# A convolution pass whose sums, stores and loads are spread over a group's steps, with the images turned first

## The reference

```python
x = x + _L0_conv_ref(_gn(x), weight, bias_term)     # depthwise 31x31, padding 15
x = x + _L1_conv_ref(_gn(x), ...)                   # window attention (7x7 windows) and an MLP
```

## Time and profile before

| | us |
|---|---|
| median of 3 runs | 5388.03 (5382.51 to 5395.19) |
| the profiled execution | 5403.44 |
| its span | 5401.6 |
| its convolution pass, until the last copy `inner` | 1191.2 |

### The profile page before, as it was taken

One profiled execution on the slowest core, in us unless ns is written; L12 is line 12 of the kernel. 1 busy time (PEld: TensorE's weight loads), 2 busy tenths in 40 slices (PEclk: granted clock), 3 DMA queues, 4 the chain that ended last, 5 costly groups with the idle time before them and its releaser, 6 DMA issues.

```text
span 5401.6 us, 225369 instructions
## 1 busy us (share of the span) xinstructions
PE 4898.2 (91%) x94576; PEld 3759.4 (70%) x94576; DVE 3825.5 (71%) x6236; ACT 3718.6 (69%) x5686; POOL 3389.0 (63%) x4559
## 2 busy tenths in 40 slices
PE   7999999987999999999999999999999999999998
PEld 6999999974666666666666666666666666666665
DVE  6888887864777776777777777777766777677774
ACT  5676766655777777777677777777766777677775
POOL 2111111114777777777777777777777777777774
PEclk9999999995999999999999999999999999999997
DMA  8888888865666666666666666666666666666662
GB/s 190 202 202 205 198 201 199 201 141 112 137 142 137 144 137 141 139 142 137 143 134 141 138 143 138 142 137 142 138 139 133 140 142 138 138 137 142 136 141 53
DMA packets 1168755, 802.28 MB, mean 149 GB/s; under 512 B 454404, under 2 KB 1142628, under 8 KB 1167652
## 3 DMA queue, kind: packets, MB, share of 16 engines
q1 hardware_dynamic: 1167748, 787.87, 66.7%
HBM read 470.41 MB, written 317.17 MB: 146 GB/s over the span
## 4 chain that ended last, share of the span: by engine, by line
PE 46%; ACT 16%; issue 9%; DVE 6%; ACTq 0%; POOL 0%; DVEq 0%; POOLq 0%
PE ps_ring L1219 9%; PE ps_pv L1152 6%; ACT L899 6%; PE ps_ring L1089 4%; PE ps_xc L1194 4%; PE ps_t L1106 4%; PE ps_ring L1211 4%; PE ps_s L1106 3%; ACT b_lg L856 3%; ACT b_mid L884 3%; PE ps_ring L1091 3%; DVE b_h L1002 3%; DVE b_rest L1013 3%; PE ps_ring L1090 3%; ACT b_rstd L861 2%
## 5 line engine op out<-in xcount | busy, mean ns | idle before, releaser
L970 DVE TENSOR_REDUCE b_mx<-ps_s 113x12 f32<-113x588 f32 x1024 | 780.8, 762 | 160.3 <-PE ps_s L1106 160.0
L869 ACT ACTIVATE b_probs_t<-ps_t 128x588 f32<-128x588 f32 x1024 | 667.0, 651 | 329.0 <-PE ps_t L1106 328.9
L775 POOL TENSOR_TENSOR b_mid_lo<-b_mid,b_mid_hi 128x392 fp32r<-128x392 f32 x768 | 788.0, 1026 | 43.2
L1152 PEld LDWEIGHTS ps_pv<-b_vd,b_probs_t 128*49 128x49 f32 x24576 | 614.9, 127 | 162.4 <-issue 153.4
L1152 PE MATMUL ps_pv<-b_vd,b_probs_t 128*49 128x18 f32 x24576 | 665.7, 200 | 0.3 <-issue 0.3
L830 POOL TENSOR_TENSOR b_outs<-b_y,b_xs 96x392 f32<-96x392 f32 x256 | 317.2, 1239 | 444.7 <-DVE b_y L1051 444.7
L856 ACT ACTIVATE b_lg<-ps_ring,b_cols 96x392 f32<-96x392 f32 x512 | 299.1, 584 | 383.4 <-PE ps_ring L1098 380.4
L1008 DVE TENSOR_TENSOR b_sq_lo<-b_sq,b_sq_hi 96x392 fp32r<-96x392 f32 x256 | 289.3, 1130 | 332.0 <-ACT b_sq_hi L877 332.0
L258 POOL TENSOR_TENSOR xd<-xt 128x448 f32<-128x448 f32 x96 | 112.1, 1168 | 649.0 <-DVE xt L409 649.0
L884 ACT ACTIVATE b_mid<-ps_ring,b_cols 128x392 f32<-128x392 f32 x768 | 424.2, 586 | 135.1 <-PE ps_ring L1091 132.1
L817 POOL TENSOR_SCALAR b_planes<-b_rest 96x784 bf16<-96x784 f32 x256 | 216.3, 845 | 421.9 <-DVE b_rest L1017 421.9
(11 more groups left out here) (166 smaller groups left out, 14196.1 us busy)
## 6 DMA issues: line engine op xcount, KB each, us to landing
stacked_qk<-b_planes SPq DMA_DIRECT2D x512, 220.5 KB, 3.0
b_q_st<-stacked_qk SPq DMA_DIRECT2D x512, 220.5 KB, 4.4
b_k_st<-stacked_qk SPq DMA_DIRECT2D x512, 220.5 KB, 5.7
toep<-filters_padded SPq DMA_DIRECT2D x96, 936.5 KB, 7.0
stacked_qk<-b_planes SPq DMA_DIRECT2D x512, 147.0 KB, 2.3
gtoep<-filters_summed SPq DMA_DIRECT2D x96, 624.5 KB, 9.3
stacked_qk<-b_planes SPq DMA_DIRECT2D x512, 73.5 KB, 1.9
b_xs<-x_scratch SPq DMA_DIRECT2D x224, 147.0 KB, 2.9
```

What stands on the lines that cost most here:

```text
L775: pool.tensor_tensor(mid_lo[:, m, :], mid[:, m, :], mid_hi[:, m, :].bitcast(F32), ALU.subtract).then_inc(S["mid_split"], 1)
L869: act.activation(pt[:, p, :].rearrange("k (e n) -> k e n", e=2), ps_t[:, :, 0:HPAIR * TOK], ACT.Exp, scale=float(DH) ** -0.5).then_inc(S[" ...
L970: dve.tensor_reduce(mx[0:rows_q, :].rearrange("q (e m p) -> q e m p", e=2, p=PAIRS)[:, :, :, p], ps_s[0:rows_q, :, 0:HPAIR * TOK].rearrang ...
L1152: ins = pe.matmul(to, pt[:, p, at:at + TOK], vd[:, m % VR, p, h, :, :], start=True, stop=True, skip_group_check=True)
```

## The change

In `conv_pass` alone:

- **ScalarE.** `stats` makes one pass for each call. The values of `xin` are summed when k = 3g-5, the squares when k = 3g-4; the values of `x1t` when k = 3g+3, the squares when k = 3g+4. Each pass now counts on `sums_done` or `sums1_done`, so those who wait for them count to twice the number.
- **SP.** The stores of a group are issued when k = 3g+4 instead of 3g+3. The loads stay where they are.
- **VectorE.** The images of channel k+2 are turned at the head of the step. The variance stands ahead of the low halves of the filters, and the shift `aff` between the two.
- **POOL.** `xd` is formed of channel k+2, a step earlier.
- **Filter semaphores.** The second filter counts on its own semaphore, `g_loaded`, and ScalarE waits for it only before its rounding.

```diff
             def load_filter(c):
...
-                for pad, dst, n in ((wpad, toep, TLEN), (gpad, gtoep, GLEN)):
+                for pad, dst, n, done in ((wpad, toep, TLEN, t_loaded), (gpad, gtoep, GLEN, g_loaded)):
...
-                    sp.dma_start(dst[:, c % TR, :], src).then_inc(t_loaded[c % TR], 16)
+                    sp.dma_start(dst[:, c % TR, :], src).then_inc(done[c % TR], 16)
...
-                g = group(k, 3)
+                g = group(k, 4)
                 if g is not None:
                     sp.wait_ge(x1_done, GC * (g + 1))
...
             def step(k):                                   # POOL
-                c = channel(k, 1)
+                c = channel(k, 2)
                 if c is not None:
                     pool.wait_ge(turned, c + 1)
...
-            def stats(src, dst, done):
-                for func, to in zip((ACT.Copy, ACT.Square), dst):
-                    if count[0]:
-                        act.wait_ge(summed, count[0])
-                    act.activation(junk[:, :, :, :], src, func, accum_out=to).then_inc(summed, 1)
-                    count[0] += 1
+            def stats(src, func, to, done):
+                if count[0]:
+                    act.wait_ge(summed, count[0])
+                act.activation(junk[:, :, :, :], src, func, accum_out=to).then_inc(summed, 1)
+                count[0] += 1
                 act.wait_ge(summed, count[0])
                 act.nop().then_inc(done, 1)
...
-                    act.wait_ge(t_loaded[c % TR], 32 * (c // TR + 1))
+                    act.wait_ge(t_loaded[c % TR], 16 * (c // TR + 1))
...
+                    act.wait_ge(g_loaded[c % TR], 16 * (c // TR + 1))
                     act.activation(by_block(gtoep_hi[:, c % 2, :]), blocks_of(gtoep[:, c % TR, :], GLEN, 2),
                                    ACT.Copy).then_inc(t_high, 1)
...
-                g = group(k, -4)
+                g = group(k, -5)
                 if g is not None:
                     act.wait_ge(x_loaded[g % XR], 192 * (g // XR + 1))
                     if g >= 2:
                         act.wait_ge(moments, g - 1)
-                    stats(xin[:, g % XR], [sums[:, g % 2, q:q + 1] for q in range(2)], sums_done)
+                    stats(xin[:, g % XR], ACT.Copy, sums[:, g % 2, 0:1], sums_done)
+                g = group(k, -4)
+                if g is not None:
+                    stats(xin[:, g % XR], ACT.Square, sums[:, g % 2, 1:2], sums_done)
                 g = group(k, 3)
                 if g is not None:
                     act.wait_ge(x1_done, GC * (g + 1))
-                    stats(x1t[:, g % 2], [sums1[:, q, g:g + 1] for q in range(2)], sums1_done)
+                    stats(x1t[:, g % 2], ACT.Copy, sums1[:, 0, g:g + 1], sums1_done)
+                g = group(k, 4)
+                if g is not None:
+                    stats(x1t[:, g % 2], ACT.Square, sums1[:, 1, g:g + 1], sums1_done)
...
             def step(k):                                   # VectorE
+                c = channel(k, 2)
+                if c is not None:
+                    g, ch = divmod(c, GC)
+                    dve.wait_ge(normed, g + 1)
+                    if c >= 2:
+                        dve.wait_ge(diffed, c - 1)
+                        dve.wait_ge(x_split, c - 1)
+                    dve.transpose(xt[:, c % 2, :, :, :].rearrange("p b y n -> p (b y n)"),
+                                  natural_blocks(xn[:, g % 2, ch, :, :].rearrange("p y s -> p (y s)"))).then_inc(
+                                      turned, 1)
                 c = channel(k, -1)
...
-                        dve.wait_ge(sums1_done, g - 1)
+                        dve.wait_ge(sums1_done, 2 * g - 2)
...
-                c = channel(k, 1)
-                if c is not None:
-                    dve.wait_ge(t_high, 2 * c + 2)
-                    if c >= 1:
-                        dve.wait_ge(conv_lo, c)
-                    dve.tensor_tensor(by_block(toep_lo[:, :]), ...)
-                    dve.tensor_tensor(by_block(gtoep_lo[:, :]), ...).then_inc(t_split, 1)
                 g = group(k, -3)
                 if g is not None:
...
                     dve.tensor_tensor(m[:, 2:3], m[:, 2:3], m[:, 1:2], ALU.add).then_inc(var_done, 1)
                 c = channel(k, 1)
                 if c is not None:
+                    dve.wait_ge(t_high, 2 * c + 2)
+                    if c >= 1:
+                        dve.wait_ge(conv_lo, c)
+                    dve.tensor_tensor(by_block(toep_lo[:, :]), ...)
+                g = group(k, -3)
+                if g is not None:
+                    m = mom[:, g % 2]
+                    dve.wait_ge(std_done, g + 1)
+                    dve.scalar_tensor_tensor(aff[:, g % 2, 1:2], m[:, 0:1], -1.0, aff[:, g % 2, 0:1], ALU.mult,
+                                             ALU.mult).then_inc(affine, 1)
+                if c is not None:
+                    dve.tensor_tensor(by_block(gtoep_lo[:, :]), ...).then_inc(t_split, 1)
+                c = channel(k, 1)
+                if c is not None:
                     dve.wait_ge(x_high, c + 1)
...
-                g = group(k, -3)                           # the shift, and the turn of channel k+2 behind it
...
             def step(k):                                   # TensorE
...
-                    pe.wait_ge(sums_done, g + 1)
+                    pe.wait_ge(sums_done, 2 * g + 2)
```

More of the change, by code:

```diff
@@ L138, in conv_pass @@
         t_loaded = [sem(f"t_loaded{r}") for r in range(TR)]
+        g_loaded = [sem(f"g_loaded{r}") for r in range(TR)]
         x1_stored = [sem(f"x1_stored{r}") for r in range(2)]
@@ L389, in step @@
                 if c is not None:
+                    dve.wait_ge(t_high, 2 * c + 2)
+                    if c >= 1:
+                        dve.wait_ge(conv_lo, c)
+                    dve.tensor_tensor(by_block(toep_lo[:, :]), blocks_of(toep[:, c % TR, :], TLEN, NDY),
+                                      by_block(toep_hi[:, c % 2, :]).bitcast(F32), ALU.subtract)
+                g = group(k, -3)
[5 more added lines that the diff above has]
+                if c is not None:
+                    dve.tensor_tensor(by_block(gtoep_lo[:, :]), blocks_of(gtoep[:, c % TR, :], GLEN, 2),
+                                      by_block(gtoep_hi[:, c % 2, :]).bitcast(F32), ALU.subtract).then_inc(t_split, 1)
+                c = channel(k, 1)
+                if c is not None:
                     dve.wait_ge(x_high, c + 1)
@@ L395, in step @@
                                       ALU.subtract).then_inc(x_split, 1)
-                g = group(k, -3)
[L397 to L411, removed]
             steps(dve, step)
-            dve.wait_ge(sums1_done, GROUPS)
+            dve.wait_ge(sums1_done, 2 * GROUPS)
             for q in range(2):
```

## The result

The changed kernel takes 5318.44 us (median of 4 runs, 5307.98 to 5322.96), the one before 5389.56 with a fourth run: 71.1 us less, a ratio of 0.9866 (95% interval 0.9847 to 0.9885). The prediction was 5317.

A forecast was written before the change was run, and what follows sets the result against it. Bound taken: TensorE in the first pass, losing 78.9 us through late `gtoep_lo`, laid to ScalarE. Minus 78.9 plus 7.9 in the start gives -71.0: 5332.4 from the profiled 5403.44, 5317 for the median; range 5306 to 5365 at 0.8.

The forecast's parts named there:

- What can be won: First pass, channel 1 to channel 95's copy: 1136.7 us against 1057.8 for undisturbed channels, so 78.9 us lost.
- one wait: TensorE's idle wait for the low half of the summed filter (`gtoep_lo`): 50.3 us in 35 waits.
- The cause of that wait: ScalarE's late copy `inner` delays VectorE, whose `gtoep_lo` then reaches TensorE late; VectorE waits 150.1 us for that copy.
- ScalarE's step of 14 us: ScalarE from copy 47 to copy 48, with variance stand and two passes: 13.99 us where TensorE takes 11.29.
- as no filter is late: Extra filter semaphore lets `toep_hi` start before the second filter lands; counted at nothing.
- VectorE's slack of about 3: With the copy on time, `gtoep_lo` is done at 7.7 us (8.2 with the variance) against 11.06: 3 to spare.
- The timetable after: Times from a group's channel start: low halves 21.0, loads issued until 10.0, next filter 21.0, ScalarE's moved sum 16.1.
- `xn` beside VectorE: POOL's normalized group `xn` now runs beside VectorE subtractions; cost bounded between none and all of its 2.92 us.
- The full addition: All 2.92 us of `xn` added to VectorE's time, with 1.3 us to spare and no cost on TensorE.
- DMA: DMA engines in the stretch: bounds nothing or 18 us, nothing taken; rival that DMA sets the pace, chance 0.15.
- The start: Program start: first rounding waits behind group 1's sum, channel 1 at 62.3 instead of 54.43; cost 7.9, ends 0 and 12.

## Why the prediction was right, and where it was not

- *What can be won.* 78.9 us, from the length of a clean channel and the count of means. Measured: 1136.73 - 1057.69 = 79.0. The step carried the forecast: the whole loss, idle and slow clock together, hung on one wait, and with it went the falls of the clock.
- *The cause of that wait* is where the prediction was wrong. It laid the delay to ScalarE's step of 14 us. That step is intact with the stores moved (13.98), and no wait is left; and with the variance early it is cut (10.52), and all the waits are left. What paced the kernel was the loop through SP. The view of waits of the kernel before had the line, ScalarE's longest wait in the stretch:

```profile
ACT toep_hi L302 <- DMA gtoep<-filters_summed: 156.6, 29, 7.5
```

  It stands above the 150.1 us of VectorE's wait for the copy, and the prediction did not take it up. It saw that the filter was issued 9.1 us late, but put no price of its own on that, and it counted the second filter semaphore at nothing "as no filter is late": alone that semaphore won 57.0 us. Copy 48 was 4.2 us late (channel 49 starts at 626.17, and a free copy 0.2 later); 2.7 of that is the step of 14 us, and 1.5 is what copy 47 was late already, in a step of ScalarE that had stood for a filter:

```profile
607.06 1.87 ACT L302 ACTIVATE toep_hi<-toep 128x1920 fp32r<-128x1920 f32 x1 [3.68 <-DMA gtoep<-filters_summed]
```

  VectorE's slack of about 3 takes the 2.7 and not the 4.2. The forecast rests on what is lost and on the timetable after, and both held, SP's queue included. That the wrong cause did no harm is luck: the change holds parts that cut the loop, beside those that were aimed at ScalarE's step.
- *The timetable after.* Low halves of the second step at 21.0, measured 604.92 - 584.01 = 20.9; the filter behind the loads at 10.0, measured 10.1; the next at 21.0, measured 20.9; ScalarE at the early sum at 16.1, measured 16.2. All four rest on durations of single instructions, added along one queue.
- *`xn` beside VectorE.* The full addition, `xn` done at 12.8; measured 591.34 + 5.37 - 584.01 = 12.7. Right in the sum, but the order was another: POOL waited for all three subtractions, none of them was stretched, and VectorE stood 2.67 us for `xn` instead. By the Trainium skill ("SBUF — State Buffer", section "Who interferes with whom") the engine that issues first keeps the shared port pair for the whole instruction and the other blocks. The trace agrees for `gtoep_lo`, which began 0.29 us ahead of `xn` (591.05 and 591.34) and kept its 1.49 us. That `xn` stayed behind `xt_lo` and `xd_lo` too, which began after it, is what this trace adds.
- *DMA.* No cost was taken; none is seen, as TensorE never waits in the stretch. The DMA share, forecast near 0.92, is 0.87.
- *The start.* Cost 7.9, channel 1 at 62.3; measured 6.4 (60.80), and 61.6 in the second profile of the same kernel. TensorE's start at 48.3 was 47.92; channel 0 was counted at 14.0 and took 12.88, since its first third took 5.3 us (to the means' product at 53.19; 5.9 in the second profile) and not 6.4.

## What to carry to other kernels

Ask of every wait who made the waiting engine late in the first place, until the chain comes back to itself; the longest wait on the engine that is blamed is the one to look at, and here one number in one queue was enough for 78.0 of 79.0 us. Where parts of a change are said to help together, run each alone: two of five were worth nothing alone, and a third, worth 25.8 us alone, only cost 8 us in the start once the others were there. Look in the start of the program separately: an order that is right in the steady state can put a load that lands late ahead of the first work.

## What the runs showed of the hardware

- POOL's `xn` took 5.37 us beside three back-to-back subtractions of two SBUF tiles on VectorE and 2.92 right behind them, while these subtractions kept their 1.49, 1.09 and 0.62. In the one overlap before both took longer: `xd` ended at 32.71 and `gtoep_lo` at 34.05, 1.34 us later and near its own 1.48, so there POOL seems to have come in ahead of a subtraction that began after it.
- The share of busy DMA time is no fixed amount of work. The same bytes took 0.85 x 1136.7 = 966 us of it before, 0.87 x 1057.7 = 920 after, and 0.92 x 1057.7 = 973 with loads and stores in one step again. The bound of the prediction that was made from it was too high by 5%.
- TensorE ran 1057.7 us without a pause at a granted clock of 1.00, with the DMA engines at 210 GB/s beside it.
